# End columns of the pooling as contiguous bf16 halves, made by ScalarE and VectorE, in a four-stage pipelined vision-tower kernel

## The reference

```
h = tok(x)                              # 3x3 depthwise convolution + bias, then the mean over 8x8 blocks: 64 tokens of 128 channels an image
h = h + attention0(layernorm(h))        # one head, softmax(q k) x
h = h + experts(layernorm(h))           # two shared experts and the two best of eight routed ones, exact gelu
h = h + attention1(layernorm(h))        # eight heads with rotary, 15 compressed keys, a sink
h = h + mixer(layernorm(h))             # two triangular 128x128 matrices with a gelu between
```

## Time and profile before

| | us |
|---|---|
| median of 3 runs | 2091.96 |
| lowest and highest | 2079.8, 2095.05 |
| the profiled execution, its time | 2071.78 |
| the profiled execution, its span | 2070.0 |
| mean granted TensorE clock in it | 0.925 of full |

### The profile page before, as it was taken

How to read it: one execution, slowest core, us unless ns; L and a number is a source line. 1 busy time by engine, 2 the same in 40 slices (tenths; PEclk the granted TensorE clock), 3 DMA queues, 4 the chain that set the end, 5 groups by cost and what they waited for, 6 DMA issues and landing times.

```text
span 2070.0 us, 47437 instructions
## 1 busy us (share of the span) xinstructions
PE 1745.7 (84%) x15216; PEld 1352.3 (65%) x15216; DVE 1268.4 (61%) x3484; ACT 948.9 (46%) x2291; POOL 950.9 (46%) x770
## 2 busy tenths in 40 slices
PE   1454879989897989899897989899897989998956
PEld 1443766868676776768676776768675776866644
DVE  2566456757675766767575766767675756753432
ACT  0122534546463645456363635445463635553522
POOL 1224245454556555464456464464445554533222
PEclk9999988989999999999898989999998989999986
DMA  6647454544544444545445444544445444301000
GB/s 245 243 163 255 179 201 167 194 154 152 203 183 168 181 168 175 199 148 192 157 178 204 181 155 155 211 158 172 165 168 209 179 136 170 131 20 50 17 26 6
DMA packets 109170, 332.08 MB, mean 160 GB/s; under 512 B 13662, under 2 KB 87585, under 8 KB 92412
## 3 DMA queue, kind: packets, MB, share of 16 engines
q1 hardware_dynamic: 86416, 300.90, 39.5%
q0 software_dynamic: 8992, 19.42, 2.9%
q10 hardware_dynamic: 13516, 8.51, 1.4%
HBM read 299.48 MB, written 29.29 MB: 159 GB/s over the span
## 4 chain that ended last, share of the span: by engine, by line
PE 65%; POOL 10%; issue 9%; DMA 7%; DVE 4%; ACT 2%; ACTq 1%; SPq 1%; POOLq 0%; DVEq 0%
PE hid_bank L598 11%; PE pool_bank L452 6%; DMA outs_d<-ys 5%; PE pool_bank L457 5%; POOL yg L1357 5%; PE sec_bank L654 4%; PE hid_bank L583 4%; PE sec_bank L674 4%; PE hid_bank L582 3%; PE sec_bank L665 3%; POOL xbuf L1346 3%; PE hid_bank L584 2%; PE sec_bank L617 2%; PE sec_bank L634 2%; PE down_bank L543 2%
## 5 line engine op out<-in xcount | busy, mean ns | idle before, releaser
L1346 POOL TENSOR_TENSOR xbuf<-xbuf 128x512 f32<-128x512 f32 x256 | 330.1, 1289 | 528.3 <-DVE xbuf L1039 518.5
L850 ACT ACTIVATE hid<-hid_bank,bias_t 128x128 f32<-128x128 f32 x960 | 273.7, 371 | 122.3 <-PE hid_bank L584 116.4
L598 PE MATMUL hid_bank<-w_s,hid 128*128 x1920 | 291.3, 297 | 0.0
L598 PEld LDWEIGHTS hid_bank<-w_s,hid 128*128 128x128 f32 x1920 | 243.8, 199 | 16.7
L1039 DVE TENSOR_TENSOR xbuf<-xbuf 128x1536 f32<-128x1536 f32 x128 | 236.7, 1849 | 25.9 <-DMA xbuf<-in_x 25.9
L582 PE MATMUL hid_bank<-xt,w_b 128*128 128x128 bf16 x960 | 201.3, 230 | 33.8 <-issue 18.4
L1060 DVE SCALAR_TENSOR_TENSOR taps<-pooled_s,tapw,taps 128x256 f32<-128x256 f32 (+1 forms) x416 | 210.0, 505 | 29.9 <-issue 21.6
L1043 DVE TENSOR_TENSOR xbuf<-xbuf 128x512 bf16<-128x512 f32 x128 | 90.3, 706 | 213.5 <-ACT xbuf L764 213.4
L1384 POOL TENSOR_TENSOR keys_h<-keys,heads 128x632 f32<-128x632 f32 x128 | 198.6, 1578 | 18.1 <-PE sec_bank L654 15.6
L1200 DVE COPY ys<-hid_bank 128x128 f32<-128x128 f32 x240 | 68.8, 287 | 219.0 <-PE hid_bank L598 192.8
L583 PE MATMUL hid_bank<-xt,w_b 128*128 128x128 bf16 x960 | 202.9, 230 | 0.1
(11 more groups left out here) (213 smaller groups left out, 3443.7 us busy)
## 6 DMA issues: line engine op xcount, KB each, us to landing
xbuf<-in_x SPq DMA_DIRECT2D x128, 2048.0 KB
rows_s<-rows_d SPq DMA_DIRECT2D x48, 320.0 KB, 8.9
outs_d<-ys SPq DMA_DIRECT2D x240, 64.0 KB
out<-h ACTq DMA_DIRECT2D x16, 256.0 KB
w_s<-in_w ACTq DMA_DIRECT2D x1, 2560.0 KB
hid<-in_w POOLq DMA_DIRECT2D x10, 256.0 KB, 3.7
rows_d<-x2r,spot_i POOLq DMA_INDIRECT x128
yg<-outs_d,spot_i POOLq DMA_INDIRECT x128
```

What stands on the lines that cost most here:

```text
L598: mm = nc.tensor.matmul(hid_bank[n % 2][:, 0:P], hid[:, n % RING, q * P:(q + 1) * P], w_q, start=False, stop=q == FC - 1)
L850: ins = nc.scalar.activation(hid[:, n % RING, cols], hid_bank[n % 2][:, cols], ACT.Gelu, bias=bias_t[:, q, j:j + 1])
L1346: nc.gpsimd.tensor_tensor(v[:, :, 1, :], v[:, :, 1, :], v[:, :, 2 * k + 3, :], ALU.add) \
```

## The change

A new kind of work, `ends.u.v`, splits columns 0 and 7 as `inner` splits the inner sum: ACT copies both columns to bf16 (into the first half of the free columns 2 and 6) as soon as `pair` is done, DVE subtracts that copy from the fp32 columns and writes the low halves behind them. The matmuls on the end columns then are pairs of bf16 matmuls with `block_b` in place of single fp32 matmuls with `block_sum`. Pieces 0 and 2 of a pool step wait for `ends_low` in place of `x_in`. The order table is written anew on all engines; two lines of it stand here.

```diff
-        tap.1.8' pair.0.0 tap.1.9' tap.1.10' tap.1.11' tap.1.12' tap.1.13' tap.1.14' inner.0.0 pair.0.1 att.0
+        tap.1.6' tap.1.7' tap.1.8' tap.1.9' tap.1.10' tap.1.11' pair.0.0 tap.1.12' tap.1.13' pair.0.1 tap.1.14'
+        ends.0.0 inner.0.0 att.0 ends.0.1 moe att.1 mix pre.1 narrow.0 inner.0.1 narrow.1 pre.2 pair.1.0 pre.3
...
+        ends_high, ends_low = sem("ends_high", 2 * T), sem("ends_low", 2 * T)
...
                     if k in (0, 2):
-                        eng.wait_ge(x_in[v], at(x_in[v], g, 16 * (u + 1)))
+                        eng.wait_ge(ends_low, at(ends_low, g, 2 * u + v + 1))
...
                         for bx in range(BX // 2):
-                            mm = nc.tensor.matmul(view[:, 1, :, side[bx]], blocks[v][:, bx, 0, :], block_sum[:],
-                                                  start=True, stop=True)
+                            for h in range(2):
+                                mm = nc.tensor.matmul(view[:, 1, :, side[bx]], halves[v][:, bx, 2, h, :], block_b[:],
+                                                      start=h == 0, stop=h == 1)
...
                         for bx in range(BX // 2):
-                            mm = nc.tensor.matmul(view[:, :, v, side[bx]], blocks[v][:, bx, 7, :], block_sum[:],
-                                                  start=True, stop=True)
+                            for h in range(2):
+                                mm = nc.tensor.matmul(view[:, :, v, side[bx]], halves[v][:, bx, 6, h, :], block_b[:],
+                                                      start=h == 0, stop=h == 1)
...
+                elif kind == "ends":
+                    eng.wait_ge(x_paired, at(x_paired, g, 2 * u + k + 1))
+                    nc.scalar.activation(halves[k][:, :, 2:7:4, 0, :], blocks[k][:, :, 0:8:7, :], ACT.Copy) \
+                      .then_inc(ends_high, 1)
...
+                elif kind == "ends":
+                    eng.wait_ge(ends_high, at(ends_high, g, 2 * u + k + 1))
+                    nc.vector.tensor_tensor(halves[k][:, :, 2:7:4, 1, :], blocks[k][:, :, 0:8:7, :],
+                                            halves[k][:, :, 2:7:4, 0, :], ALU.subtract).then_inc(ends_low, 1)
```

More of the change, by code:

```diff
@@ L46 @@
 STAGES = ("tok", "att", "ffn", "sec")
-STAGE_OF = dict(pair="tok", add="tok", inner="tok", pool="tok", tap="tok", out="tok",
+STAGE_OF = dict(pair="tok", add="tok", inner="tok", ends="tok", pool="tok", tap="tok", out="tok",
                 att="att", low="att", high="att", rest="att", scatter="att", up="ffn", hidden="ffn", down="ffn", moe="ffn",
@@ L61 @@
     pe="""
-        up.0 up.1 table up.2 down.0 up.3 down.1 up.4 up.5 down.2 out' up.6 down.3 down.4 pool.0.0 pool.0.1
-        pool.0.2 up.7 down.5 down.6 att.1 down.7 att.2 lift.0 pool.0.3 lift.1 widen.0 widen.1 lift.2 att.3
-        narrow.0 pre.2 narrow.1 lift.3 widen.2 att.4 pre.3 lift.4 narrow.2 lift.5 pool.1.0 pre.4 pool.1.1 widen.3
-        pre.5 pre.6 pre.7 widen.4 narrow.3 score.0 pool.1.2 score.1 pool.1.3 lift.6 att.7 score.2 score.3 widen.5
-        lift.7 score.4 score.5 narrow.4 score.6 score.7 att.8 widen.6 lift.8 narrow.5 turn.0 widen.7 turn.1
@@ L81 @@
-    dve="""
-        tap.1.8' pair.0.0 tap.1.9' tap.1.10' tap.1.11' tap.1.12' tap.1.13' tap.1.14' inner.0.0 pair.0.1 att.0
-        inner.0.1 att.1 mix moe pre.1 pre.2 pair.1.0 narrow.0 pre.5 inner.1.0 pre.3 narrow.1 att.4 pre.4 att.5
-        pair.1.1 gate att.7 narrow.2 narrow.3 inner.1.1 score.0 score.1 pair.2.0 score.2 score.3 score.4 score.5
-        narrow.4 score.6 score.7 att.8 tap.0.0 narrow.5 tap.0.1 inner.2.0 tap.0.2 tap.0.3 pair.2.1 att.9 tap.0.4
-        narrow.6 value.0 inner.2.1 tap.0.5 tap.0.6 value.1 tap.0.7 att.10 value.2 tap.0.8 narrow.7 tap.0.9
-        tap.0.10 value.3 rest tap.0.11 pair.3.0 value.4 narrow.8 att.11 value.5 narrow.9 inner.3.0 value.6
-        pair.3.1 value.7 tap.0.12 narrow.10 att.12 post.1 narrow.11 post.2 inner.3.1 narrow.12 tap.0.13 post.3
-        tap.0.14 low narrow.13 narrow.14 tap.1.0 tap.1.1 tap.1.2 tap.1.3 tap.1.4 tap.1.5 tap.1.6 tap.1.7 post.5
-        weights.0 weights.1 weights.2 weights.3 weights.4 weights.5 weights.6 weights.7 weights.8 weights.9""",
+        up.0 table up.1 down.0 up.2 down.1 up.3 up.4 down.2 up.5 up.6 down.3 down.4 out' up.7 down.5 pool.0.0
@@ new lines @@
+        down.6 pool.0.1 down.7 lift.0 widen.0 lift.1 pool.0.2 widen.1 lift.2 att.1 narrow.0 narrow.1 lift.3
+        widen.2 pool.0.3 att.2 lift.4 pre.2 widen.3 pre.3 att.3 lift.5 narrow.2 att.4 pre.4 narrow.3 pre.5 lift.6
+        pre.6 pool.1.0 pool.1.1 pre.7 widen.4 score.0 score.1 att.7 score.2 lift.7 narrow.4 pool.1.2 score.3
+        pool.1.3 score.4 widen.5 lift.8 score.5 score.6 score.7 lift.9 att.8 narrow.5 widen.6 turn.0 widen.7
+        lift.10 turn.1 value.0 pool.2.0 narrow.6 turn.2 value.1 pool.2.1 narrow.7 att.10 turn.3 pool.2.2 value.2
@@ new lines @@
+        pool.2.3 att.11 widen.8 turn.4 widen.9 value.3 turn.5 narrow.8 lift.11 value.4 turn.6 value.5 narrow.9
+        turn.7 widen.10 value.6 widen.11 value.7 narrow.10 att.12 lift.12 post.0 narrow.11 pool.3.0 post.1
+        lift.13 pool.3.1 widen.12 lift.14 widen.13 narrow.12 pool.3.2 widen.14 narrow.13 pool.3.3 post.3
+        narrow.14 post.4 post.5""",
+    act="""
+        table hidden.0 hidden.1 hidden.2 hidden.3 hidden.4 hidden.5 ends.0.0 ends.0.1 inner.0.0 out' hidden.6
+        hidden.7 pool.0.0 lift.0 inner.0.1 lift.1 widen.0 widen.1 lift.2 lift.3 att.1 widen.2 att.2 pre.2 lift.4
+        widen.3 att.3 pool.0.2 gate ends.1.0 pool.0.3 lift.5 inner.1.0 pre.5 lift.6 pre.6 att.6 ends.1.1 pre.7
+        widen.4 inner.1.1 pool.1.0 lift.7 pool.1.2 pool.1.3 att.7 widen.5 lift.8 exp lift.9 ends.2.0 turn.0
+        inner.2.0 widen.6 turn.1 widen.7 ends.2.1 pool.2.0 turn.2 inner.2.1 att.10 high turn.3 widen.8 turn.4
+        pool.2.2 lift.10 turn.5 widen.9 lift.11 turn.6 pool.2.3 ends.3.0 turn.7 widen.10 inner.3.0 widen.11
+        post.0 ends.3.1 lift.12 lift.13 pool.3.0 inner.3.1 widen.12 lift.14 widen.13 widen.14 post.3 pool.3.2
+        pool.3.3 post.4 post.5 weights.0 weights.1 weights.2 weights.3 weights.4 weights.5 weights.6 weights.7
+        weights.8 weights.9""",
@@ L96 @@
+        add.0.3 pre.1 add.1.0 add.1.1 pre.3 pre.4 pre.6 pre.7 add.1.2 add.1.3 score.2 score.4 add.2.0 add.2.1
+        att.9 add.2.2 add.2.3 add.3.0 add.3.1 add.3.2 add.3.3 scatter.0 post.1 scatter.1 post.2 scatter.2
+        scatter.3 scatter.4 scatter.5 scatter.6 scatter.7 weights.0 weights.1 weights.2 weights.3 weights.4
         weights.5 weights.6 weights.7 weights.8 weights.9""")
```

32 lines of the change are left out of this document (12 added, 20 removed).

## The result

The changed kernel takes 2174.96 us in the median (2170.95 to 2188.18, 4 runs), beside 2085.88 for the kernel before on the same chip: ratio 1.044, 95% interval 1.037 to 1.051. It is slower by 4.4%; the forecast was 1979. The profiled execution took 2170.95, its span is 2169.2 us. One run stands far off in what follows: of the tenth experiment's four, one took 2776.6 us beside 1935.8 to 1943.9; it is in the median given there, not in the ratio.

The account below looks back on a forecast made before the run. PE, busy 91% of steady turns, was taken as the bound. Savings of 110.5 (turns 3 to 15), 7 (turn 2) and 10 (turns 0, 1) less 14.3 (DVE) made 113.2 us: 2092.0 to 1979, range 1915 to 2055.

Parts of the forecast that it names:

- Removed from PE: End-column matmuls on PE as bf16 instead of fp32: 8.5 us a turn saved, 110.5 us over turns 3 to 15.
- What pooling costs PE, the turn pays: Steady turns: pooling adds 19.6 us of PE work and 21.2 us of turn, so PE was taken as the bound.
- Turn 16: Turn near the end without pooling or loads, 94.7 us: claimed the other stages' latency chains hold no turn above that.
- Turn 2 and turns 0 and 1: First turns: 7 us saved in turn 2, and 10 us in turns 0 and 1 with ends 0 and 16.8.
- Added to ACT: Eight copies a turn on ACT, 1.06 us each, 8.5 us a turn, beside POOL's additions; no cost in the sum.
- Added to DVE: Eight subtractions a turn on DVE, 1.28 us each, 10.2 us; PE's waits grow 1.1 us a turn, 14.3 in thirteen.
- slower: the subtractions wait in DVE's row: On DVE, each subtraction waits for ACT's copy; a turn gets 8.2 us longer, 2182 us; chance 0.10.
- Moved: Reordered work, such as `pool.0.2` and `att.1` further back in PE's row: nothing given for `mix`.
- The clock: On PE, one more low-clock stretch a turn takes 26 us of the gain: 2005 us, left inside the range.
- The 107 us that I named as the sign: Sign of a right forecast: line 857 recurring at some 107 us in turns 3 to 15.

Follow-up runs that it names:

- the tenth experiment: Kernel before, old order, end columns as upper 16 bits read in place twice, lower halves left out, POOL's additions cut to 16 of 128 channels: 1942.89 us, ratio 0.932.
- The fifth experiment: Kernel before, old order, end columns multiplied as upper 16 bits read in place twice, lower halves left out, nothing added on ACT or DVE: 2036.17 us, ratio 0.974.
- the third: Changed kernel, new order, without DVE's eight subtractions a turn; low halves left out, high halves multiplied twice: 2071.62 us, ratio 0.994.
- the first experiment: Kernel before, code untouched, with the new order table less its `ends` entries: 2199.98 us, ratio 1.055.
- the twelfth: Kernel before, old order, end columns multiplied once as upper 16 bits read in place, lower bits left out, nothing added on any engine: 2024.07 us, ratio 0.967.
- the ninth experiment: Changed kernel in the old order with upper halves alone: ACT's copies placed early, no subtraction, low halves left out: 2058.66 us, ratio 0.988.

## Why the prediction was wrong

The table takes PE's turn apart: busy time by its granted clock gives the work at full clock (good to about 1 us: the clock has two digits, and kernels with the same matmuls come out at 97.4 to 98.4 and at 88.1 to 89.8), the rest of the busy time is what the lower clock adds, and then the idle time. All in us a turn.

| kernel | turn | PE work at full clock | lower clock adds | PE idle |
|---|---|---|---|---|
| before | 115.9 | 98.4 | 7.4 | 10.1 |
| new order alone | 123.1 | 97.7 | 12.1 | 13.3 |
| new order, ends made, fp32 kept | 134.7 | 97.4 | 19.9 | 17.3 |
| after | 122.0 | 89.1 | 12.1 | 20.7 |
| after without the subtraction | 115.1 | 89.8 | 8.9 | 16.4 |
| old order, ends placed by hand | 120.8 | 89.4 | 11.0 | 20.4 |
| old order, PE's saving alone | 113.6 | 88.1 | 7.7 | 17.9 |
| the same, small additions | 108.0 | 88.1 | 5.6 | 14.4 |

*Removed from PE: the size was right, the worth was not.* The pieces take 0.21 us as said (1085.38, 1085.59, 1085.79 are the starts of three in a row), and PE's work at full clock fell by 8.6 to 10.3 us a turn. The step that failed is "What pooling costs PE, the turn pays". I read 91% busy, and 1.3 us idle in 76, as a bound. The fifth experiment gives 2.3 us a turn for it, 30 us of 110.5 (by the medians, 54.8 us less the 11.8 ahead of turn 2, at most 3.3 a turn). PE was full, but the path through stores, gathers, additions and x was as good as full too, 2 to 3 us behind; the 10.1 us of idle time in each turn was its sign. I read that idle time from one row, the 2.93 us for x, yet x has only 13.7 of its 131 us; the largest wait in the same stretch is for ACT's h, and I did not follow it:

```profile
PE pool_bank L449 <- ACT h L782: 43.7, 9, 6.5
```

What the saving is worth depends on the table: in the new order, with ACT's copies already added, it gave 8.0 us a turn (the third against the first experiment). Turn 16, which I took as proof that the latency chains fit into 94.7 us, has neither loads nor additions and so says nothing of the chain that matters with them. The tenth experiment shows POOL's additions on that chain; the gathers and the stores were not shortened, so their part in it is read from the trace alone.

*Turn 2 and turns 0 and 1.* The fifth experiment's mark of turn 2 stands at 193.7 in place of 205.5: 11.8, where I had 10. That size was right for PE's saving alone; in the changed kernel the mark comes at 207.0, so the added work took it all back. Turn 2 gave 1.2 in the fifth experiment and not 7, and is 5.0 longer in the changed kernel.

*Added to ACT, costs nothing.* The copy lasts 1.05 us as said, but in the old order its price is 2.0 us a turn: the twelfth against the ninth experiment, and in the ninth PE waits 33.0 us in thirteen turns for it. In the changed kernel no row of PE waits for the copy directly, and its price there was not measured.

*Added to DVE.* Mis-sized twice. An instruction lasts 1.63 us in the turns, not 1.28, because POOL's instructions hold it up; and DVE's work rose by 16.5 us a turn, not 10.2, since other instructions are held too. That second part comes mostly with the table: the new order alone has DVE at 81.9 us, 4.0 more than before, and the third experiment, without a subtraction, at 84.4. From there to the changed kernel it is 10.1, which is my 10.2 by luck: the subtractions take 13.0, and others were held less. I had priced it from the mean rows of other DVE instructions, with no word on DVE and POOL meeting. The price is 6.9 us a turn in the new order (122.0 less 115.1), and 4.9 in the old one (120.8 less the ninth's 115.9, with the low matmuls and three moved pieces in it), where I took 1.1 with 8.5 as the end of the range. The rival *slower: the subtractions wait in DVE's row* had the right side and place, but its mechanism, a wait for ACT's copy, is small: the new subtraction waits 9.2 us for it in thirteen turns. They fill the row; they do not wait in it. The long waits at `pool.0.0`, 63 us, are a third thing, POOL's additions behind six gathers; without the subtractions PE waits 41 us there.

*Moved: nothing.* The new table costs the unchanged kernel 7.2 us a turn. For the changed kernel nothing shows it to blame: with the ends placed by hand the old table gives 120.8, the new one 122.0, and without the subtractions the two are alike. Which of its moves does the harm while PE is full stays open.

*The clock.* I had left a further fall inside the range. In PE's busy time it took back 4.7 of the 9.3 us that PE's work at full clock lost; how much of that is also time of the turn is not shown, since PE waits more as well. PE stands idle from 1048.2 to 1055.6, waiting for line 1052, and is granted the lower level (1.2 GHz) for nearly all of the next four us of work:

```profile
1055.59 0.48 PE L452 MATMUL pool_bank<-block_b,xbuf 128*128 128x48 bf16 x8 [7.38 <-DVE xbuf L1052]
```

```profile
1052.00:1056.00 4.00, 0.41 (x11) 0.44 (x12) 1.20 (x5) 1.86 (x4) 3.47 (x4) 0.62 0.07 23
1056.00:1060.00 4.00, 4.00 (x34) 3.94 (x31) 2.84 (x9) 0.89 (x2) 3.87 (x4) 0.52 0.33 72
```

In the table the kernels with full PE work show it best: 13.3 us idle go with 12.1 lost to the clock, 17.3 with 19.9. The relieved kernels follow less closely (17.9 with 7.7, 16.4 with 8.9). That the idle causes the fall is what the rows suggest; no experiment changed the clock alone.

*The sum as measured,* in us a turn and in the old order: minus 2.3 for PE, plus 2.3 for ACT's copies (the ninth against the fifth), plus 4.9 for DVE's subtractions: 4.9 more than before, against 7.4 less in the forecast (8.5 less 1.1). The 107 us that I named as the sign leaves DVE's term out; the sum makes it 108.5.
